# An attention block with a routed expert layer: the first batch's places made inside the attention, one shared pass in front of the expert tiles

## The reference

```
h = layernorm(x) * (1 + ca) + sa
x = x + ga * attention(h)            # 32 query heads, 8 key/value heads of 8, causal
h = layernorm(x) * (1 + cb) + sb
probs = softmax(h @ w_router)        # 16 experts
top_w, top_i = top_k(probs, 4); top_w = top_w / sum(top_w)
routed = sum over the 4 chosen e of top_w * (silu(h @ we1[e]) * (h @ we3[e])) @ we2[e]
shared = (silu(h @ ws1) * (h @ ws3)) @ ws2       # hidden width 512
x = x + gb * (shared / 5 + routed * 4 / 5)
```

## Time and profile before

| | us |
|---|---|
| median of three runs | 837.43 (836.93 to 844.99) |
| the profiled execution | 833.49 |
| its span | 831.7 |
| PE busy | 726.1 (87%) |
| DVE busy | 604.7 (73%) |
| ACT busy | 457.0 (55%) |
| POOL busy | 263.2 (32%) |

### The profile page before, as it was taken

How to read it: one execution, slowest core, us unless ns; L and a number is a source line. 1 busy time by engine, 2 the same in 40 slices (tenths; PEclk the granted TensorE clock), 3 DMA queues, 4 the chain that set the end, 5 groups by cost and what they waited for, 6 DMA issues and landing times. The chain is left out here.

```text
span 831.7 us, 14406 instructions
## 1 busy us (share of the span) xinstructions
PE 726.1 (87%) x4894; PEld 432.2 (52%) x4894; DVE 604.7 (73%) x1126; ACT 457.0 (55%) x784; POOL 263.2 (32%) x350
## 2 busy tenths in 40 slices
PE   8659699999999999999999988878699998889761
PEld 7336344444444444444444454766578886667551
DVE  7538878989999999899998463664765557774267
ACT  4122157788777778777777656144456654443110
POOL 6300014323322232233332111473077037300643
PEclk9869679999999999999999988999999999999996
DMA  6657105355555444434551002942278567634313
GB/s 210 182 113 229 36 17 117 78 169 169 154 171 172 129 124 147 151 90 104 145 130 38 17 14 82 320 143 71 90 235 260 163 188 228 199 122 137 104 57 95
DMA packets 78890, 112.28 MB, mean 135 GB/s; under 512 B 15780, under 2 KB 59620, under 8 KB 76708
## 3 DMA queue, kind: packets, MB, share of 16 engines
q1 hardware_dynamic: 68884, 81.67, 35.2%
q0 software_dynamic: 9280, 29.11, 10.5%
q10 hardware_dynamic: 656, 0.59, 0.4%
HBM read 59.92 MB, written 50.99 MB: 133 GB/s over the span
## 5 line engine op out<-in xcount | busy, mean ns | idle before, releaser
L790 ACT ACTIVATE probs<-psum 128x1024 f32<-128x1024 f32 (+3 forms) x384 | 289.7, 816 | 125.3 <-PE psum L965 123.1
L1119 DVE TENSOR_REDUCE max_parts<-psum 128x8 f32<-128x1024 f32 (+2 forms) x192 | 235.2, 1225 | 58.6 <-PE psum L939 55.1
L979 PE MATMUL psum<-probs,v_aug 128*32 128x512 f32 (+3 forms) x1536 | 167.0, 508 | 0.3 <-POOL probs L663 0.3
L663 POOL TENSOR_SCALAR_AFFINE_SELECT probs<-probs 128x512 f32<-128x512 f32 x128 | 81.2, 634 | 262.2 <-ACT probs L790 262.2
L965 PE MATMUL psum<-qs,ks 64*128 64x512 f32 (+3 forms) x768 | 158.2, 411 | 2.3 <-ACT probs L790 1.9
L965 PEld LDWEIGHTS psum<-qs,ks 64*128 64x128 f32 x768 | 73.7, 190 | 128.8 <-ACT probs L790 112.5
L1126 DVE TENSOR_REDUCE max_parts<-psum 128x1 f32<-128x512 f32 x192 | 130.7, 681 | 0.0
L939 PE MATMUL psum<-km,qs 64*128 64x128 f32 (+2 forms) x704 | 93.3, 336 | 31.7 <-DMA km<-k_parts 20.9
L1456 PE MATMUL psum<-w_all,v_aug 128*128 x376 | 99.1, 386 | 2.8 <-DVE wmod_sb L1564 2.0
L939 PEld LDWEIGHTS psum<-km,qs 64*128 64x128 f32 x704 | 58.0, 192 | 55.0 <-DVE max_parts L1119 21.3
L951 PE MATMUL psum<-km,qs 64*128 64x512 f32 x192 | 85.1, 443 | 0.2
(11 more groups left out here) (172 smaller groups left out, 845.5 us busy)
## 6 DMA issues: line engine op xcount, KB each, us to landing
v_aug<-x_sorted SPq DMA_DIRECT2D x94, 128.0 KB, 2.3
y_sorted<-v_aug SPq DMA_DIRECT2D x94, 128.0 KB
km<-k_parts SPq DMA_DIRECT2D x62, 160.0 KB
x_sorted<-g_rows POOLq DMA_DIRECT2D x6, 1536.0 KB, 9.5
y_sums<-g_sign SPq DMA_DIRECT2D x32, 256.0 KB, 4.9
qs<-q_parts SPq DMA_DIRECT2D x62, 128.0 KB
ks<-k_parts SPq DMA_DIRECT2D x64, 64.0 KB
w_all<-in_L_ffn_we_dram SPq DMA_DIRECT2D x16, 256.0 KB, 5.8
```

The costliest lines, as they stand in the source:

```text
L663: pool.affine_select(out=tile, in_=tile, compare_op=ALU.is_ge, fill=0.0, base=0, pattern=[[0, REP], [1, P]], channel_multiplier=-1).then_i ...
L790: act.activation(probs[s % (LAG + 1)][:, 2 * hh:2 * hh + 2, off:TT], psum[:, 2 * hh:2 * hh + 2, off:TT], ACT.Exp, scale=SCALE).then_inc(p_ ...
L979: last = pe.matmul(bank[sum_bank][32 * h:32 * h + 32, off:TT], v_aug[:, group, c, :], probs[s % (LAG + 1)][:, h, off:TT], start=(c == 0), ...
L1119: dve.tensor_reduce(out=max_parts[:, :, h0:h1, slice(*tiles), slot], in_=psum[:, wide_bank:wide_bank + 2, :].rearrange("p a (s w) -> p (a ...
```

## The change

- **Batch 0's positions move into the attention.** DVE's list of the first block now ends with `counted`, `weights`, `late_reciprocals(0)`, `totals`, `firsts` and `places`. PE's `ranks` stands at step 9 of group 15, writing the second half of the logits' bank. ACT's Exp comes one step earlier (6), and the output pairs two steps earlier (6 to 9 of group 14).
- **Four shared passes in front of the tiles, twelve behind** (`FRONT` = `NS`). Before it was eight and eight. `down` writes each quarter into banks of its own.
- **Batch 1's router goes into tiles 0 and 1 of the loop**, and its routing is cut into single operations at tiles 2 to 15 (`best`, two halves of `best_at`, `chosen`, `counted`, `weights`, two halves of `totals`, `firsts`, `places`, `experts`). Its logits have a bank of their own; its Exp stands after tile 3 on ACT.
- **A combine is taken apart.** ACT makes the first product (`combine_begin`); DVE does one of the remaining operations after each tile (`combine_part`), the last two together. The first stands at tile 58 instead of 55. The second batch's combines stand whole at passes 7, 8, 9, 11, 12, 13 and 14, the last after the passes.
- **The variance's two halves are separate functions**; in the second block `low(2)` on DVE stands between them, and on ACT `high(q)` directly follows `shared_silu(q)`.

In the diff a context of one line stands around each change; left out are `variances` and `deviations`, the wait and the bank added in `router` and the waits of `down`, and leading spaces are shortened.

```diff
@@ -214,20 +217,26 @@
...
+
+    def best_at(self, dve, link, tiles):
         settled(dve)
-        for j in range(TC):
+        for j in tiles:
             ins = dve.max_index(top_i[:, j, :], self.top[:, j, :], self.lg[:, j, :])
...
+
+    def chosen(self, dve, link):
         link(dve.tensor_copy(self.top_f, top_i[:]))
-
-    def chosen(self, dve, link):
         dve.wait_ge(consts_s, 8)
...
+
+    def counted(self, dve):
         dve.tensor_reduce(out=self.hits, in_=self.hit.rearrange("p j r e -> p j e r"), axis=AX.X, op=ALU.add)\
...
+
+    def weights(self, dve, link):
         link(dve.tensor_reduce(out=self.wsum, in_=self.top[:, :, 0:TOPK], axis=AX.X, op=ALU.add))
@@ -241,13 +250,16 @@
...
+    def totals(self, dve, link, psum_ranks, tiles):
+        counts = psum_ranks[:, P:2 * P].rearrange("p (j e) -> p j e", e=E)
+        if 0 in tiles:
+            link(dve.memset(self.upto[:, 0, :], 0.0))
+            dve.wait_ge(rank_full, self.b + 1)
+        for j in tiles:
+            link(dve.tensor_tensor(out=self.upto[:, j + 1, :], in0=counts[:, j, :], in1=self.upto[:, j, :], op=ALU.add))
+
...
-        counts = psum_ranks[:, P:2 * P].rearrange("p (j e) -> p j e", e=E)
-        link(dve.memset(self.upto[:, 0, :], 0.0))
-        dve.wait_ge(rank_full, self.b + 1)
-        for j in range(TC):
-            link(dve.tensor_tensor(out=self.upto[:, j + 1, :], in0=counts[:, j, :], in1=self.upto[:, j, :], op=ALU.add))
         link(dve.tensor_tensor(out=self.over, in0=self.upto[:, TC, :].unsqueeze(2).to_broadcast([P, E, TC]),
@@ -780,7 +793,7 @@
...
                     square_roots(act, 0, var2, sqrt2)
-                if group == GROUPS - 1 and s == 7:
+                if group == GROUPS - 1 and s == 6:
                     act.wait_ge(lg_ready, 1)
@@ -1000,12 +1013,14 @@
...
-            if group == GROUPS - 2 and 8 <= s < 12:
-                output_pair(s - 8)
+            if group == GROUPS - 2 and 6 <= s < 10:
+                output_pair(s - 6)
             elif group == GROUPS - 1 and s in (1, 2):
...
                 router(pe, s - 2)
+            elif group == GROUPS - 1 and s == 9:
+                route[0].ranks(pe, bank[lg_banks[0]][:, 2 * P:4 * P])
@@ -1189,11 +1207,18 @@
...
         dve.wait_ge(lg_full, 2)
-        route[0].logits(dve, chain.link, bank[lg_bank][:, 0:P].rearrange("p (j e) -> p j e", e=E))
-
+        route[0].logits(dve, chain.link, bank[lg_banks[0]][:, 0:P].rearrange("p (j e) -> p j e", e=E))
+
+        ranked = bank[lg_banks[0]][:, 2 * P:4 * P]
         route[0].best(dve, chain.link)
+        route[0].best_at(dve, chain.link, range(TC))
         route[0].chosen(dve, chain.link)
+        route[0].counted(dve)
+        route[0].weights(dve, chain.link)
         late_reciprocals(dve, 0)
+        route[0].totals(dve, chain.link, ranked, range(TC))
+        route[0].firsts(dve, chain.link, ranked)
+        route[0].places(dve, chain.link)
         core.close()
@@ -1225,13 +1250,15 @@
...
     "tile_turned", "tile_shifted", "tile_up", "tile_silu", "tile_mult", "tile_g_turned", "tile_g_read", "tile_down", "tile_y_copied")]
-        rows_in_s, combined, o_out = [sem(f"rows_gathered_{k}") for k in range(NG)], sem("combined"), sem("out_written")
+        rows_in_s, begun_s, combined, o_out = [sem(f"rows_gathered_{k}") for k in range(NG)], sem("combine_begun"), sem("combined"), sem("out_written")
         X_BANKS, U_BANKS, G_BANK, Y_BANKS = (0, 1), (2, 3), 4, (6, 7)
-        UP_BANKS, DOWN_BANKS = (0, 1), (2, 2, 2, 4)
+        UP_BANKS, DOWN_BANKS = (0, 1), (2, 2, 4, 6)
         AHEAD_T, STORE_LAG = 2, 8
-        RANK_AT, FIRST_COMBINE = 4, TILES + 8
-
-        FRONT, STEPS_S = 2 * NS, NPASS * NS
+
+        LATE_COMBINE = [7, 8, 9, 11, 12, 13, 14]
+        RANK_AT, FIRST_COMBINE = 9, TILES + 11
+
+        FRONT, STEPS_S = NS, NPASS * NS
@@ -1342,27 +1369,43 @@
...
-        for q in range(FRONT):
-            shared_silu(q)
-            if q:
-                high(q - 1)
-            if q == 2:
-                square_roots(act, 1, var2, sqrt2)
-            elif q in (4, 5):
-                h2_of(q - 1)
-        high(FRONT - 1)
-        act.wait_ge(lg_ready, 2)
-        act.activation(route[1].lg, route[1].lg, ACT.Exp).then_inc(lg_exp, 1)
+        def combine_begin(n):
+            b, j = n // TC, n % TC
+            act.wait_ge(rows_in_s[n % NG], 16 * TOPK * (n // NG + 1))
+            if n >= 2:
+                act.wait_ge(combined, n - 1)
+            act.activation(acc[:, n % 2, :], rows[n % NG][:, 0, :], ACT.Copy, scale=wts[:, b, j, 0:1]).then_inc(begun_s, 1)
+
+        shared_silu(0)
+        high(0)
+        shared_silu(1)
+        high(1)
+        shared_silu(2)
+        high(2)
+        square_roots(act, 1, var2, sqrt2)
+        shared_silu(3)
+        high(3)
+        h2_of(3)
+        h2_of(4)
         for i in range(-AHEAD_T, NTILE):
...
                 shifted_rows(i + AHEAD_T)
+            if i == 3:
+                act.wait_ge(lg_ready, 2)
+                act.activation(route[1].lg, route[1].lg, ACT.Exp).then_inc(lg_exp, 1)
+            if i >= FIRST_COMBINE - 1 and (i - FIRST_COMBINE + 1) % 4 == 0 and (i - FIRST_COMBINE + 1) // 4 < TC:
+                combine_begin((i - FIRST_COMBINE + 1) // 4)
         for q in range(FRONT, STEPS_S):
...
                 high(q - 1)
+            if q in LATE_COMBINE:
+                combine_begin(TC + LATE_COMBINE.index(q))
         high(STEPS_S - 1)
+        for n in range(len(LATE_COMBINE), TC):
+            combine_begin(TC + n)
@@ -1490,18 +1530,8 @@
...
         turned_x(pe, 3)
-        up(4)
+        turned_x(pe, 4)
         down(3)
-        turned_x(pe, 4)
-        up(5)
-        down(4)
-        router(pe, 3)
-        up(6)
-        down(5)
-        router(pe, 4)
-        up(7)
-        down(6)
-        down(7)
         for i in range(-AHEAD_T, NTILE + 2):
@@ -1511,8 +1541,10 @@
...
                 turned_g(i - 1)
-            if i == RANK_AT:
-                route[1].ranks(pe, bank[rank_banks[1]])
+            if i in (0, 1):
+                router(pe, 3 + i)
+            elif i == RANK_AT:
+                route[1].ranks(pe, bank[lg_banks[1]][:, 2 * P:4 * P])
         for q in range(FRONT, STEPS_S):
@@ -1583,51 +1615,44 @@
...
-        def combine(n):
+        def combine_part(n, part):
             b, j = n // TC, n % TC
             a = acc[:, n % 2, :]
-            dve.wait_ge(rows_in_s[n % NG], 16 * TOPK * (n // NG + 1))
-            link(dve.tensor_scalar(a, rows[n % NG][:, 0, :], wts[:, b, j, 0:1], None, ALU.mult))
-            for r in range(1, TOPK):
-                link(dve.scalar_tensor_tensor(out=a, in0=rows[n % NG][:, r, :], scalar=wts[:, b, j, r:r + 1], in1=a,
+            if part == 0:
+                dve.wait_ge(begun_s, n + 1)
+            if part < TOPK - 1:
+                link(dve.scalar_tensor_tensor(out=a, in0=rows[n % NG][:, part + 1, :], scalar=wts[:, b, j, part + 1:part + 2], in1=a,
                                               op0=ALU.mult, op1=ALU.add))
-            link(dve.tensor_tensor(out=a, in0=a, in1=gate[:, 1, b, :], op=ALU.mult))
-            dve.wait_ge(shared_done, 4)
-            dve.tensor_tensor(out=x_sb[:, n, :], in0=x_sb[:, n, :], in1=a, op=ALU.add).then_inc(combined, 1)
+            else:
+                link(dve.tensor_tensor(out=a, in0=a, in1=gate[:, 1, b, :], op=ALU.mult))
+                dve.tensor_tensor(out=x_sb[:, n, :], in0=x_sb[:, n, :], in1=a, op=ALU.add).then_inc(combined, 1)
+
+        def combine(n):
+            for part in range(TOPK):
+                combine_part(n, part)
...
         late_reciprocals(dve, 1)
-        route[0].firsts(dve, link, bank[rank_banks[0]])
-        route[0].places(dve, link)
         residual(3)
...
         shared_mult(1)
-        route[0].experts(dve, link)
         low(1)
...
         shared_mult(2)
-        deviations(dve, link, 1, var2, sqrt2)
+        variances(dve, link, 1, var2)
         low(2)
+        deviations(dve, link, 1, sqrt2)
         normal(dve, 3)
...
         low(3)
-        shared_mult(4)
+        route[0].experts(dve, link)
         shared_sum(0)
-        low(4)
-        shared_mult(5)
-        low(5)
         late_low(3)
-        shared_mult(6)
-        low(6)
         late_low(4)
-        shared_mult(7)
-        dve.wait_ge(lg_full, NPASS)
-        route[1].logits(dve, link, bank[lg_bank][:, P:2 * P].rearrange("p (j e) -> p j e", e=E))
-        low(7)
-        shared_sum(1)
+        ranked = bank[lg_banks[1]][:, 2 * P:4 * P]
         for i in range(NTILE + 2):
@@ -1635,30 +1660,40 @@
...
                 turned_out(i - 1)
-            if i == RANK_AT - 3:
+            if i == 2:
+                dve.wait_ge(lg_full, NPASS)
+                route[1].logits(dve, link, bank[lg_banks[1]][:, 0:P].rearrange("p (j e) -> p j e", e=E))
+            elif i == RANK_AT - 5:
                 route[1].best(dve, link)
+            elif i in (RANK_AT - 4, RANK_AT - 3):
```

(32 more changed lines are left out.)

31 lines of the change are left out of this document (17 added, 14 removed).

## The result

The changed kernel took 835.42 us in the median of 18 runs (831.96 to 841.91), the kernel before 838.64 in 18 runs on the same chip. The ratio is 0.9956, with a 95% interval from 0.9936 to 0.9976: 3.7 us less, where 6.2 were forecast. The profiled execution took 832.14 us with a span of 830.4, against 833.5 and 831.7 before. So this pair differs by 1.3 us, and it is this pair that can be taken apart.

The account below looks back on a forecast made before the run. It took PE as the bound in attention and tiles, passes then sort before the tiles, and DVE alone at the end. Its terms summed to -6.2, from 837.4 to 831.2 us; forecast's own range 827 to 836, overall 822 to 840.

Parts of the forecast that it names:

- the clock's term: First tiles: after the long idle PE runs at its lower clock for a while; +1.7 us, between 0 and 4.
- The router's groups: Tiles 0 and 1: the second batch's 32 router matmuls move from the front into the loop; +3.7 us.
- Tiles' start: Before the tiles: the earlier sort brings the first transpose 17.8 us forward; from there to first `up_rows`, another -1.2.
- Combines: Tile loop: split combines no longer delay PE, so all 8 x 1.45 us go; -11.6.
- the parts lengthen the tiles: Rival, tile loop: each combine part adds its length to the tile; sum becomes +12.8, 850 us; chance 0.1.
- GpSimd's slowed sort: Rival, before the tiles: DVE operations hold each of the sort's 32 issues; +15.5, 846.7 us; chance 0.05.
- Second Exp: Tile loop, ACT: the second Exp with two table loads moves into the loop; +1.5 us, between 0 and 2.9.
- Routing in single steps: Tile loop: second batch's routing, cut into steps, costs 5.0 us instead of 7.5; -2.5, between -7.5 and +2.
- Four more passes, and sum and combine in one pass: Behind the tiles: four unhidden passes, +23.7 us; `shared_sum` followed by a combine delays PE twice, +3.0, between +1 and +5.
- Tail: End of the span: combine work leaves the stretch where DVE is alone; -6.7 us, between -4 and -7.
- more is hidden: Rival, tile loop: routing steps, Exp and slow clock cost nothing; 823.0 us; chance 0.2.

Follow-up runs that it names:

- Fill: The changed kernel plus 52 unread identity products on TensorE behind the last down products in front of the tiles; 827.9 us, 0.9850 of the kernel before.
- Late places: The changed kernel with the first batch's rank products and places back in the second block, as in the kernel before; 848.34 us, 1.0138 of the kernel before.
- the best kernel: The changed kernel with eight passes in front, low part before the next product, both router groups before `up(7)`, banks and late combines rearranged; 796.77 us, 0.9512 of the kernel before.

## Why the prediction was wrong

The direction, the range (822 to 840) and the mechanism were right: the sort became the wait in front of the tiles, and moving the passes and bringing the sort forward gave and took about the same. Every sign that the prediction named came out (first write at 517.23, 43.2 us to the first load, 13.6 us of idle, 6.73 for four tiles, 5.93 a pass, 8.6 at the end). The size of the saving was not: 6.2 us forecast, 3.7 measured, and 1.3 in the profiled pair, which the sum was made for.

- **The failed step is the clock's term.** The prediction put it as "some 1.5 are lost. I take +1.7, between 0 and 4", from the earlier trace rows, a row after 4.1 us of waiting in the middle of dense passes. Fill measures it: 7.5 us in the tiles. That is 5.8 too little, more than the whole error of 4.9, and outside the bounds. That the sum missed by no more, and that the time lies within the forecast's own range, is luck: with 7.5 in place of 1.7 the sum would have been -0.4, no saving; the routing's steps gave back 1.2. The row gave the depth of the dip correctly (products at twice their time) but nothing on its length: there the dip cost 1.5 us in all, here it lasted 16. The router's groups, which the same change puts into tiles 0 and 1, were costed at full clock (3.7), and took 3.43 each in the dip.
- **Tiles' start** -17.8, measured -18.1; the late end of the block (1.9 us for 2.1), the 43.4 of the sort (43.2) and the load (2.1 for 2.3) came as forecast. From the first transpose to the first up product 1.7 us passed, 0.9 less than before, where 1.2 less was forecast. Late places shows that this chain is the path: 11.6 us.
- **Combines** -11.6, measured 11.9 by undoing them. The rival "the parts lengthen the tiles" is out, and GpSimd's slowed sort too: from the first scattered write to the first load 43.2 us.
- **Second Exp** +1.5; one wait of 1.80, some 2 us in all. The Trainium skill ("ScalarE: Activation LUTs", "What ACT_TABLE_LOAD costs") adds 1.38 us of drain to a switch; the trace has load, Exp and load at 581.21, 582.51 and 582.84 back to back and nothing between them, so the row was the better price.
- **Routing in single steps** -2.5; from the up products of tile 6 (586.04) to those of tile 18 (610.14) are 24.1 us where twelve tiles need 20.3: 3.8 is left of 7.5, so -3.7. The steps in tiles 2 to 5 lie under the low clock and are not in that.
- **Four more passes, and sum and combine in one pass** +23.7 and +3.0; together with what follows them +28.1. The first is exact (5.93 each). The second costs up to 4.4, because the low clock after a wait of 3.71 reaches into the next pass. **Tail** -6.7, measured -6.8.

The chances: the time is within 1% of before (0.53), in the forecast's own range of 827 to 836 (0.5). The rival "more is hidden", at 0.2, had the clock cost nothing; that it could cost far more had no rival at all.

## What to carry to other kernels

When a change opens an idle stretch in front of TensorE's densest part, price the stretch twice: once as idle time, and once as what comes after it at half clock, to be read from what will run there and not from a short dip elsewhere. If the idle time can't be filled with work, products that nobody reads gave 9 us here; where there is no idle time to fill, as on the slower chips, they stand on the path themselves. Before work is moved from one side of a loop to the other, ask what it covered: the other parts of this change were worth 21 us more with the passes left in front. And a wait of the same length in each of many passes is an order to be changed: making the low part ahead of the next product took a swap of two lines on two engines and gave 11 us.

## What the runs showed of the hardware

- The granted clock fell to 0.50 in an idle stretch of 7.67 us as in one of 13.60 and of 22.25, and didn't in one of 2.03. How long it stayed low in the tiles went with what ran there: 16.4 us behind the first transpose with the router's groups, 6.4 without, although TensorE was busy in nearly all of that time (14.9 of the 16 us from 562 to 578). And in the best kernel it fell with no idle time at all (8.00 of 8 us busy from 555 to 563), during 16 router products in a row. The Trainium skill ("TensorE: Matmul & The Clock Gate", "What's actually happening") says that the low level is the default and that activity releases it. The traces agree in that the long idle stretches were followed by the low level; that activity releases it is not enough to foresee 16.4 us of low clock under a busy engine, or its fall in the best kernel.
- A dip can follow waits of 3.71 us between dense passes, and its length differs from pass to pass and trace to trace: the pass after such a wait took 8.55 and 7.47 us in one trace, 7.22 and 7.24 in another.
- Three chips ran every version of this program some 10% slower (the kernel before 925, 926 and 932 us, 838 to 840 on the others), with other waits. Ratios between kernels that differ in order alone moved too (the best kernel 0.951 on one chip, 0.971 and 0.970 on two of those). Compare on one chip.
